# Two groups of products become turns, and four engines get a new order of calls

## The chip, the cores and the metric

The kernel runs on one core of a Trainium2 chip, in one launch. The metric is the device time of that launch in microseconds (us); several runs of the same program are taken, and their median counts. The core has five engines that work side by side, each through its own list of instructions in order: TensorE (PE, which multiplies and transposes into PSUM), VectorE (DVE), ScalarE (ACT), GpSimd (POOL) and SyncE (SP, which here starts transfers). They wait for each other by semaphores.

## The reference

Input x is 16 sequences of 256 tokens of 128 numbers. Two layers follow each other, each on the layer norm of its input, and each added to it:

```
step(params, x):                              # scanned over the 16 sequences
    z, y  = x @ t_k.T, x @ t_v.T
    grads = grad(mean((recon(params, z) - y)**2))     # recon(z) = z + gelu(z @ W1.T + b1) @ W2.T + b2
    params = params - 0.001 * grads
    return params, recon(params, x @ t_q.T)

ffn(x):                                       # each sequence by itself
    x = x + proj(attention(rope(qkv(rmsnorm(x)))))    # 16 heads, 4 of keys, window of 128, a sink
    h2 = rmsnorm(x)
    top 4 of 32 experts per token; x + sum of weight * (silu(h2 @ g) * (h2 @ u)) @ down
```

The parameters go from one sequence to the next, so the steps of the first layer can't run side by side. Everything is in f32.

## The kernel before, in words

After the loads the program has two parts. `layers` runs a loop that is written out over n = -1 to 20; `experts` follows when all engines have left it, and computes the chosen experts over 160 tiles of 128 rows, which GpSimd has sent to DRAM by expert during the loop.

An iteration of the loop works on five sequences at once, each in another stage. Stage F (sequence n) is the step of the first layer: turn the normed rows xn into columns (`x_turn`), `z_products`, `a_products`, then the gradient through `z_rows`, `residual_cols`, `residual_rows`, `hidden_grad` and `gradients`, which DVE's `update` adds to the weights in `fast`, `fast2` and `b1`. Stage O (n - 1) makes the layer's output with the new weights. Stage N (n - 2) makes q, k and v in six chunks (`chunk`, `rope`, `rope_add`, `qk_turn`). Stage A (n - 3) is attention in six units of heads (`scores`, `maxima`, `exps`, `scaled`, `turn_probs`, `take_probs`, `values`, `take_y`); its last units run on into the next iteration. Stage B (n - 4) projects, picks experts and sends rows. All stages are at work from n = 4 to 15, the first ones alone in n = 0 to 2, the last ones alone in n = 16 to 19.

The stages are functions for each engine. What sets the order is `iteration` of each engine: a list of calls, run through from top to bottom. A call waits on semaphores for the calls of other engines that it reads from or whose buffer it takes over, so a call that waits holds up all that stands behind it on its engine. Matrices in the column layout have a token per column (zT, rT, hT2), in the row layout a token per partition (z, r, h). The gradients need z and the residual r in the row layout: `z_rows` (L449) and `residual_rows` (L472) make them in PSUM, and DVE copies them out (`a_rows`, `slope_cdf`). zT is copied out by ACT's `zT_out` (L1176) before `a_products`, rT by `rT_out` (L1196) after `residual_cols`.

`idle` is a product of zeros that PE runs in the first three iterations and the last. `first_stats` makes the statistics of the input on DVE in iteration 0, in passes of four tiles; pass 3 waits for the load of x, pass 4 makes constants. ACT loads a table of functions when it goes from exponentials to Gelu and Tanh and back, twice an iteration.

Of the kernel before, what the change touches and what calls it, by code (L numbers as in the profile page):

```python
# [24 lines left out]
P = 128  # L25
# [201 lines left out]
def layers(m):  # L227
# [12 lines left out]
    with ExitStack() as ctx:  # L240
# [112 lines left out]
        def _(pe):  # L353
# [283 lines left out]
            def iteration(n, par):  # L637
                project(n, par, 1, 0)
                qk_turn(n - 1, 1 - par, 5)
                norm_turn(n - 1, 1 - par)  # L640
                values(n - 1, 1 - par, 4)
                idle(n, par, 0)
                turn_probs(n - 1, 1 - par, 5, 0)
                x_turn(n, par)
                chunk(n, par, 0)
                z_products(n, par)
                idle(n, par, 1)
                idle(n, par, 2)
                scores(n, par, 1)
                turn_probs(n - 1, 1 - par, 5, 1)  # L650
                qk_turn(n, par, 0)
                project(n, par, 1, 1)
                idle(n, par, 3)
                a_products(n, par)
                chunk(n, par, 1)
                values(n - 1, 1 - par, 5)
                turn_probs(n, par, 0, 0)
                scores(n, par, 2)
                turn_probs(n, par, 0, 1)
                z_rows(n, par)  # L660
                qk_turn(n, par, 1)
                project(n, par, 0, 0)
                project(n, par, 0, 1)
                chunk(n, par, 2)
                values(n, par, 0)
                turn_probs(n, par, 1, 0)
                scores(n, par, 3)
                idle(n, par, 4)
                turn_probs(n, par, 1, 1)
                residual_cols(n, par)  # L670
                idle(n, par, 5)
                qk_turn(n, par, 2)
                values(n, par, 1)
                residual_rows(n, par)
                chunk(n, par, 3)
                turn_probs(n, par, 2, 0)
                h2_turn(n, par)
                scores(n, par, 4)
                idle(n, par, 6)
                idle(n, par, 7)  # L680
                turn_probs(n, par, 2, 1)
                hidden_grad(n, par)
                gate(n, par)
                idle(n, par, 8)
                idle(n, par, 9)
                qk_turn(n, par, 3)
                values(n, par, 2)
# [5 lines left out]
                idle(n, par, 10)  # L693
                qk_turn(n, par, 4)
                values(n, par, 3)
                ranks(n, par)
                idle(n, par, 11)
                chunk(n, par, 5)
                turn_probs(n, par, 4, 0)
                scores(n + 1, 1 - par, 0)  # L700
                gradients(n, par)
                turn_probs(n, par, 4, 1)
# [9 lines left out]
        def _(v):  # L712
# [298 lines left out]
            def iteration(n, par):  # L1011
                recips(n - 1, 1 - par, 5)
                scaled(n - 1, 1 - par, 5, 0)
                scaled(n - 1, 1 - par, 5, 1)
                rope(n, par, 0)
# [4 lines left out]
                scaled(n, par, 0, 0)  # L1020
                scaled(n, par, 0, 1)
                sinks(n, par, 1)
                first_stats(n, par, 3)
                rope(n, par, 1)
                first_stats(n, par, 4)
                a_bias(n, par)
                slots(n - 1, 1 - par)
                maxima(n, par, 2)
                shifts(n, par, 2)
                sinks(n, par, 2)  # L1030
                first_stats(n, par, 5)
                sums_out(n, par, 1)
                centred(n, par)
                a_rows(n, par)
                recips(n, par, 1)
                scaled(n, par, 1, 0)
                attended(n, par)
                scaled(n, par, 1, 1)
                rope(n, par, 2)
                sums_out(n, par, 2)  # L1040
                maxima(n, par, 3)
                recips(n, par, 2)
                shifts(n, par, 3)
                sinks(n, par, 3)
                scaled(n, par, 2, 0)
                h2_rows(n, par)
                scaled(n, par, 2, 1)
                first_stats(n, par, 6)
                slope_pdf(n, par)
                slope_cdf(n, par)  # L1050
                rope(n, par, 3)
                sums_out(n, par, 3)
                first_stats(n, par, 7)
                maxima(n, par, 4)
                shifts(n, par, 4)
                first_stats(n, par, 8)
                recips(n, par, 3)
                hidden_grad(n, par)
                pick(n, par)
                sinks(n, par, 4)  # L1060
                first_stats(n, par, 9)
                scaled(n, par, 3, 0)
                scaled(n, par, 3, 1)
                rope(n, par, 4)
                sums_out(n, par, 4)
                maxima(n, par, 5)
                recips(n, par, 4)
                shifts(n, par, 5)
                one_hot(n, par)
                output(n, par)  # L1070
                scaled(n, par, 4, 0)
                scaled(n, par, 4, 1)
                rope(n, par, 5)
                sinks(n, par, 5)
                places(n, par)
                maxima(n + 1, 1 - par, 0)
                first_stats(n, par, 10)
                shifts(n + 1, 1 - par, 0)
                update(n, par)
                normed_rows(n, par)  # L1080
                sinks(n + 1, 1 - par, 0)
                x_norm(n + 1, 1 - par)
# [44 lines left out]
        def _(act):  # L1127
# [122 lines left out]
            def iteration(n, par):  # L1250
                hT_out(n - 1, 1 - par)
                take_y(n - 1, 1 - par, 4)
                sink_terms(n, par, 0)
                xT_out(n, par)
                exps(n, par, 0, 1)
                take_probs(n - 1, 1 - par, 5, 0)
                v_out(n, par, 0)
# [3 lines left out]
                exps(n, par, 1, 0)  # L1261
                sink_terms(n, par, 1)
                v_out(n, par, 1)
                take_y(n - 1, 1 - par, 5)
                exps(n, par, 1, 1)
                take_probs(n, par, 0, 0)
                take_probs(n, par, 0, 1)
                qk_out(n, par, 1)
                exps(n, par, 2, 0)
                exps(n, par, 2, 1)  # L1270
                sink_terms(n, par, 2)
                take_y(n, par, 0)
                gelus(n, par)
                take_probs(n, par, 1, 0)
                take_probs(n, par, 1, 1)
                rT_out(n, par)
                qk_out(n, par, 2)
                sink_terms(n, par, 3)
                exps(n, par, 3, 0)
                exps(n, par, 3, 1)  # L1280
                take_y(n, par, 1)
                take_probs(n, par, 2, 0)
                h2T_out(n, par)
# [4 lines left out]
                weights(n, par)  # L1288
                exps(n, par, 4, 1)
                take_y(n, par, 2)  # L1290
# [4 lines left out]
                take_y(n, par, 3)  # L1295
                exps(n, par, 5, 1)
                take_probs(n, par, 4, 0)
                take_probs(n, par, 4, 1)
                sink_terms(n, par, 5)
                exps(n + 1, 1 - par, 0, 0)  # L1300
                qk_out(n, par, 5)

# [3 lines left out]
        def _(pool):  # L1306
# [81 lines left out]
            def iteration(n, par):  # L1388
                rope_add(n, par, 1)
                send(n, par, 0)  # L1390
                send(n, par, 1)
                rms2(n, par)
                rope_add(n, par, 2)
                rope_add(n, par, 3)
                send(n, par, 2)
# [3 lines left out]
                last_sends(n, par)  # L1399
                send(n, par, 3)  # L1400
                rope_add(n + 1, 1 - par, 0)
                spread(n, par)
# [400 lines left out]
```

## Time and profile before

| | |
|---|---|
| median of three runs | 1043.11 us (1042.41 to 1044.05) |
| the profiled execution's own time | 1046.03 us |
| its span, first to last instruction | 1044.3 us |
| mean granted PE clock | 0.936 |
| PE busy | 888.1 us (85% of the span) |
| DVE, ACT, POOL busy | 684.2, 602.2, 488.0 us |
| loop, to about | 777 us |

The profile is of one execution; "busy" adds up the time in which an engine had an instruction under way. PE works with two sequencer steps that overlap, the load of weights (PEld) and the product (PE). The granted clock is the share of full speed that PE was given: 1.00 is 2.4 GHz, 0.50 is 1.2 GHz. In a list of instructions a row gives start, duration, engine, line, operation, output and inputs, count, and in brackets the idle time ahead of it with what ended it. A row with x4 covers four records.

### The profile page before, as it was taken

Reading aid. Unit: us, or ns where it says so; the run is one execution under the profiler, and the core shown is the slowest. Engines: PE = TensorE matmul, PEld = TensorE weight load, DVE = VectorE, ACT = ScalarE, POOL = GpSimd, SP = SyncE. Lnnn points to the kernel's source line nnn. Section 1 sums busy time; section 2 is a strip of 40 time slices with the busy share of each in tenths; the row PEclk is TensorE's granted clock in tenths of the full one; section 3 lists DMA queues with packets and bytes.
Section 4 is the critical chain, followed back from the end, with each engine's and each line's share of the span. In section 5 each row is a group of like instructions: output and inputs, shape, how many; then the busy total and the mean of one; then the engine's idle time right before and its main releaser. Section 6 shows DMA issues by size and latency. Waiting matters only on the chain. (4 is left out here: it accounts for less than half of the span.)

```text
span 1044.3 us, 21755 instructions
## 1 busy us (share of the span) xinstructions
PE 888.1 (85%) x6865; PEld 674.9 (65%) x6865; DVE 684.2 (66%) x2456; ACT 602.2 (58%) x1987; POOL 488.0 (47%) x643
## 2 busy tenths in 40 slices
PE   3788999999999999999999999999945997777500
PEld 1455777777777777777777777776734886666400
DVE  2645877878788787887877878788742443333208
ACT  1114776767767677676776767877812654444300
POOL 2123313444444443444444444455451777777750
PEclk8788999999999999999999999999966999999855
DMA  6989999999500000000000000000002544432139
GB/s 159 268 273 375 375 374 376 368 370 368 152 13 18 15 10 18 12 18 16 10 17 13 18 15 9 18 18 18 24 33 70 135 133 132 122 105 75 52 110 331
DMA packets 98370, 131.52 MB, mean 126 GB/s; under 512 B 15025, under 2 KB 54866, under 8 KB 98258
## 3 DMA queue, kind: packets, MB, share of 16 engines
q1 hardware_dynamic: 84690, 108.36, 31.5%
q0 software_dynamic: 9216, 19.68, 5.4%
q10 hardware_dynamic: 4352, 2.10, 0.7%
q8 instruction: 57, 0.93, 0.4%
q14 instruction: 55, 0.45, 0.1%
HBM read 30.34 MB, written 99.75 MB: 125 GB/s over the span
## 5 line engine op out<-in xcount | busy, mean ns | idle before, releaser
L1315 POOL TENSOR_TENSOR l_t_cos<-l_t_cos,l_t_sin 128x512 f32<-128x512 f32 (+1 forms) x96 | 104.5, 1088 | 279.3 <-DVE l_t_sin L908 278.6
L1148 ACT ACTIVATE l_prob<-l_score,l_nm 128x128 f32<-128x128 f32 (+1 forms) x512 | 210.3, 432 | 4.1 <-DVE l_nm L767 3.9
L1521 POOL DMA_INDIRECT expert_out<-e_yo,e_dest x160 | 153.7, 960 | 69.4 <-issue 36.9
L756 DVE TENSOR_REDUCE l_mx<-l_score 128x2 f32<-128x512 f32 (+1 forms) x192 | 123.6, 686 | 70.6 <-PE l_score L379 69.0
L94 POOL DMA_INDIRECT expert_rows<-h,slot x128 | 129.6, 1013 | 56.7 <-issue 33.3
L1158 ACT COPY l_probT<-l_turned 128x512 f32<-128x512 f32 x192 | 110.9, 594 | 77.3 <-PE l_turned L393 77.1
L393 PE MATMUL l_turned<-ident_sb,l_prob 128*128 128x128 f32 x768 | 120.8, 283 | 0.4 <-DVE l_prob L741 0.3
L393 PEld LDWEIGHTS l_turned<-ident_sb,l_prob 128*128 128x128 f32 x768 | 83.3, 142 | 48.6 <-issue 43.6
L1148 ACT ACTIVATION_READ_ACCUMULATOR l_prob<-l_score,l_nm 128x1 f32 x512 | 111.3, 217 | 0.0
L379 PE MATMUL l_score<-l_kT,l_qT 64*128 64x128 f32 (+1 forms) x1024 | 110.1, 344 | 0.0
L408 PE MATMUL l_turned<-l_probT,l_vv 128*64 128x128 f32 x1536 | 105.0, 279 | 1.7 <-ACT l_probT L1158 1.5
L408 PEld LDWEIGHTS l_turned<-l_probT,l_vv 128*64 128x64 f32 x1536 | 81.9, 136 | 35.2 <-issue 31.5
L379 PEld LDWEIGHTS l_score<-l_kT,l_qT 64*128 64x128 f32 x1024 | 75.3, 187 | 44.0 <-issue 41.1
L1662 ACT ACTIVATE e_yo<-e_p_y,e_mine 128x128 f32<-128x128 f32 x160 | 45.7, 368 | 88.9 <-DMA expert_out<-e_yo,e_dest 80.1
L555 PE MATMUL l_side_q<-wqkv_sb,l_hT 128*128 128x512 f32 x186 | 96.7, 602 | 0.0
L904 DVE TENSOR_TENSOR l_t_cos<-l_side_q,rope_sb 128x512 f32<-128x512 f32 (+1 forms) x93 | 55.6, 598 | 50.5 <-PE l_side_q L555 50.3
L1603 DVE COPY e_hidT<-e_p_h 128x512 f32<-128x512 f32 x40 | 27.7, 691 | 83.7 <-PE e_p_h L1729 79.1
L1719 PE MATMUL e_p_up<-wup_sb,e_xT 128*128 x320 | 80.1, 396 | 0.0
L741 DVE TENSOR_SCALAR l_prob<-l_prob,l_rec 128x256 f32<-128x256 f32 x256 | 76.0, 354 | 0.6
L1738 PE MATMUL e_p_y<-wdown_sb,e_hidT 128*128 x320 | 45.6, 286 | 31.0 <-ACT e_yo L1662 29.0
L588 PE MATMUL l_side_g<-wproj_sb,l_yT 128*128 128x128 f32 x512 | 66.7, 278 | 0.0
L1719 PEld LDWEIGHTS e_p_up<-wup_sb,e_xT 128*128 128x128 f32 x320 | 60.9, 201 | 7.3
(235 smaller groups left out, 1785.8 us busy)
## 6 DMA issues: line engine op xcount, KB each, us to landing
expert_rows<-zeros SPq DMA_DIRECT2D x32, 2240.0 KB, 22.5
e_xt<-expert_rows SPq DMA_DIRECT2D x160, 70.0 KB
e_rows<-expert_out SPq DMA_DIRECT2D x16, 512.0 KB, 5.9
wup_sb<-in_wup SPq DMA_DIRECT2D x1, 4096.0 KB, 14.5
expert_out<-e_yo,e_dest POOLq DMA_INDIRECT x160
expert_rows<-zeros SPq DMA_DIRECT2D x32, 70.0 KB, 2.2
expert_rows<-zeros SPq DMA_DIRECT2D x4, 560.0 KB, 11.7
expert_rows<-h,slot POOLq DMA_INDIRECT x128, 2.4
```

Of the source, the lines that this page charges most:

```text
L94: m["nc"].gpsimd.indirect_dma_start(m["xs"], bass.IndirectOffsetOnAxis(ap=m["slot"][:, par, c:c + 1], axis=0), m["h2"][:, par, c // TOPK, ...
L379: ins = mm(bank[h][:, i * w:(i + 1) * w], qT[rows, ap, p, tok], kT[rows, ap, g2, 0:w], start=False, stop=(i == len(pairs) - 1))
L393: ins = tr(turned[h][:, k * P:(k + 1) * P], prob[:, u % 2, h, k * P:(k + 1) * P], ident[:])
L408: ins = mm(turned[1][h * DH:(h + 1) * DH, i * P:(i + 1) * P], vv[:, A % 3, k, g * DH:(g + 1) * DH], probT[:, h, blk * P:(blk + 1) * P], st ...
L555: mm(dst[:], hT[:, t * P:(t + 1) * P], m["wqkv"][:, part * 512:(part + 1) * 512], start=False, stop=True).then_inc(s["qkv_ps"], 1)
L741: ins = V.tensor_scalar(prob[:, b, h, j * TOK:(j + 1) * TOK], prob[:, b, h, j * TOK:(j + 1) * TOK], rec[:, b, h, j:j + 1], None, ALU.mult)
L756: V.tensor_reduce(mx[:, b, h, 0:w], score[(2 * u + h) % 3][:].rearrange("p (j k) -> p j k", j=w), AX.X, ALU.max).then_inc(s["mx"], 1)
L1148: ins = A_.activation(prob[:, b, h, cols], score[(2 * u + h) % 3][:, cols], ACT.Exp, bias=nm[:, b, h, j:j + 1], scale=0.125, accum_out=sum ...
L1158: A_.copy(probT[:, h, :], turned[h][:]).then_inc(s["probT"], 1)
L1315: g.tensor_tensor(t_cos[:, c % 2, 0:w], t_cos[:, c % 2, 0:w], t_sin[:, c % 2, 0:w], ALU.add).then_inc(s["added"], 1)
L1521: g_.indirect_dma_start(m["ys"], bass.IndirectOffsetOnAxis(ap=dest[:, g % FOUND, j:j + 1], axis=0), yo[:, g % YO, j, :], None).then_inc(se ...
L1719: ins = mm(p_up[g % 2][:, j, :], xT[:, g % 2, j, :], m["wup"][:, bass.ds(expert(g, j) * (2 * DFF), 2 * DFF)], start=True, stop=True)
```

## The change

`z_rows` and `residual_rows` take the rows from the column layouts that are there already, by turning them (a transpose on PE against the identity), where they were computed a second time by products:

```
@@ z_rows, residual_rows
                 for t in range(TPS):
-                    mm(side_f[:, TOK + t * P:TOK + (t + 1) * P], xnT[:, par, t * P:(t + 1) * P], m["tkT"][:],
-                       start=True, stop=True)
+                    tr(side_f[:, TOK + t * P:TOK + (t + 1) * P], zT[:, 0, t * P:(t + 1) * P], ident[:])
...
                 for t in range(TPS):
-                    dst, tok = side_f[:, TOK + t * P:TOK + (t + 1) * P], slice(t * P, (t + 1) * P)
-                    mm(dst, xnT[:, par, tok], dkvT[:], start=True, stop=False)
-                    mm(dst, hT2[:, 0, tok], fast2[:], start=False, stop=True)
+                    tr(side_f[:, TOK + t * P:TOK + (t + 1) * P], rT[:, t * P:(t + 1) * P], ident[:])
```

The lists of calls of all four engines are in another order. The turn of the iteration is also elsewhere: calls that stood at its head for the sequence before now stand at its end, and the other way round. Of the lists, the rows that the text speaks of:

```
@@ PE, iteration: moved to the end
-                project(n, par, 1, 0)
-                qk_turn(n - 1, 1 - par, 5)
-                norm_turn(n - 1, 1 - par)
-                values(n - 1, 1 - par, 4)
...
                 gradients(n, par)
+                ranks(n, par)
+                values(n, par, 4)
+                qk_turn(n, par, 5)
+                norm_turn(n, par)
+                project(n + 1, 1 - par, 1, 0)
@@ DVE, iteration: x_norm from the end to the head, behind first_stats(n, par, 3)
+                first_stats(n, par, 3)
+                sinks(n, par, 0)
+                x_norm(n, par)
                 recips(n - 1, 1 - par, 5)
...
-                sinks(n + 1, 1 - par, 0)
-                x_norm(n + 1, 1 - par)
@@ POOL, iteration
-                rope_add(n, par, 1)
                 send(n, par, 0)
...
                 rope_add(n + 1, 1 - par, 0)
+                rope_add(n + 1, 1 - par, 1)
```

On PE, in the middle of a full iteration, from the turn of unit 1 to the score of unit 4 (l_turned is a turn of probabilities or, from l_probT, `values`; l_side_q a chunk; l_side_f stage F). Before:

```order
L572 MATMUL l_side_q<-ident_sb,l_t_cos 128x128 x4
L408 MATMUL l_turned1<-l_probT,l_vv 64x128 x8
L479 MATMUL l_side_f<-l_dkvT,l_xnT 128x128
L480 MATMUL l_side_f<-fast2,l_hT2 128x128
L479 MATMUL l_side_f<-l_dkvT,l_xnT 128x128
L480 MATMUL l_side_f<-fast2,l_hT2 128x128
L482 MATMUL l_side_f<-ident_sb,l_hT2 128x128 x2
L357 MATMUL l_side_q<-bias3_bf,ones_bf 128x512
L555 MATMUL l_side_q<-wqkv_sb,l_hT 128x512
L393 MATMUL l_turned0<-ident_sb,l_prob 128x128 x4
L598 MATMUL l_side_g<-ident_sb,h2 128x128 x2
L373 MATMUL l_score2<-mask2,ident_bf 128x512
```

And now, from the turn of unit 1 (its second half) on:

```order
L393 MATMUL l_turned1<-ident_sb,l_prob 128x128 x4
L357 MATMUL l_side_q<-bias3_bf,ones_bf 128x512
L552 MATMUL l_side_q<-wqkv_sb,l_hT 128x512
L393 MATMUL l_turned0<-ident_sb,l_prob 128x128 x4
L408 MATMUL l_turned1<-l_probT,l_vv 64x128 x8
L595 MATMUL l_side_g<-ident_sb,h2 128x128 x2
L477 MATMUL l_side_f<-ident_sb,l_rT 128x128 x2
L479 MATMUL l_side_f<-ident_sb,l_hT2 128x128 x2
L373 MATMUL l_score2<-mask2,ident_bf 128x512
```

The four products of `residual_rows` are two turns of rT, and `h2_turn` (L595) stands between them and `values`.

On ACT, at the head of an iteration, from the copy of xnT to the copies after zT (L1148 and L1145 are `exps`, L1158 and L1155 `take_probs`). Before:

```order
L1174 COPY l_xnT<-l_side_f 128x256 [waits l_xT_ps]
L1148 ACTIVATE l_prob,l_sums<-l_score,l_nm 128x256 [waits l_t_ps,l_nm]
L1148 ACTIVATE l_prob,l_sums<-l_score,l_nm 128x256
L1158 COPY l_probT<-l_turned 128x512 [waits l_y_ps,l_t_ps]
L1218 COPY l_vv<-l_side_q 128x256 [waits l_y_ps,l_sin]
L1182 COPY l_zT<-l_side_f 128x512 [waits l_z_ps]
L1228 COPY l_kT<-l_side_q 128x2x128 [waits l_qk_ps]
L1158 COPY l_probT<-l_turned 128x512 [waits l_y_ps,l_t_ps]
```

And now:

```order
L1171 COPY l_xnT<-l_side_f 128x256 [waits l_xT_ps]
L1164 COPY l_yT<-l_turned 128x2x128 [waits l_y_ps]
L1145 ACTIVATE l_prob,l_sums<-l_score,l_nm 128x256 [waits l_t_ps,l_nm]
L1145 ACTIVATE l_prob,l_sums<-l_score,l_nm 128x256
L1215 COPY l_vv<-l_side_q 128x256 [waits l_y_ps,l_sin]
L1155 COPY l_probT<-l_turned 128x512 [waits l_y_ps,l_t_ps]
L1179 COPY l_zT<-l_side_f 128x512 [waits l_z_ps]
L1225 COPY l_kT<-l_side_q 128x2x128 [waits l_qk_ps]
```

The copy of l_probT for unit 5 has come to stand right ahead of zT; on PE its turn has moved from ahead of `x_turn` to behind `scores(1)`.

On DVE, at the start of iteration 0 (L790 and L787 are `x_norm`, L1088 and L1085 with x_all the statistics). Before:

```order
L790 TENSOR_SCALAR l_xn<-x_all,l_mv,l_rstd 128x128 [waits l_rs0]
L790 TENSOR_SCALAR l_xn<-x_all,l_mv,l_rstd 128x128
L1088 BN_STATS l_stats<-x_all 128x6 [waits x_loaded]
L1088 BN_STATS l_stats<-x_all 128x6 x3
L1091 BN_AGGR l_mv<-l_stats 128x2 [waits l_stat0]
L1091 BN_AGGR l_mv<-l_stats 128x2 x3
```

And now:

```order
L1085 BN_STATS l_stats<-x_all 128x6 [waits x_loaded]
L1085 BN_STATS l_stats<-x_all 128x6 x3
L1088 BN_AGGR l_mv<-l_stats 128x2 [waits l_stat0]
L1088 BN_AGGR l_mv<-l_stats 128x2 x3
L787 TENSOR_SCALAR l_xn<-x_all,l_mv,l_rstd 128x128 [waits l_rs0]
L787 TENSOR_SCALAR l_xn<-x_all,l_mv,l_rstd 128x128
```

`x_norm` of the first sequence stands behind the wait for the whole of x and four tiles of statistics.

## Rows read from the trace of the kernel before

**Rows 1.** Busy time by stretch: iteration 3, iterations 4 to 14, iteration 15.
```profile
core 0: us, PE busy (x) PEld busy (x) DVE busy (x) ACT busy (x) POOL busy (x), PEclk, DMA share, GB/s
91.29:133.10 41.81, 41.34 (x307) 29.30 (x308) 30.25 (x101) 29.14 (x102) 9.35 (x15) 0.93 1.03 375
...
133.10:611.17 478.07, 478.07 (x4018) 361.26 (x4016) 385.54 (x1416) 349.91 (x1200) 213.55 (x308) 1.00 0.34 118
...
611.17:654.63 43.46, 43.46 (x368) 32.83 (x366) 34.70 (x127) 31.81 (x111) 20.23 (x29) 1.00 0.04 14
```

**Rows 2.** Instructions in order of time, PE: `z_rows`, `residual_rows` of iteration 9.
```profile
404.88 0.61 PE L455 MATMUL l_side_f<-tkT_sb,l_xnT 128*128 128x128 f32 x4
405.33 0.38 PE L458 MATMUL l_side_f<-ident_sb,l_aT 128*128 128x128 f32 x2
...
414.85 0.49 PE L479 MATMUL l_side_f<-l_dkvT,l_xnT 128*128 128x128 f32 x2
415.17 0.39 PE L480 MATMUL l_side_f<-fast,l_hT 128*128 128x128 f32 x2
...
415.84 0.38 PE L482 MATMUL l_side_f<-ident_sb,l_hT 128*128 128x128 f32 x2
416.06 0.38 PE L357 MATMUL l_side_q<-bias_bf,ones_bf 128*128 128x512 bf16 x1
```

**Rows 3.** The same view, PE: calls that stand ahead of the two joints.
```profile
397.62 0.65 PE L393 MATMUL l_turned<-ident_sb,l_prob 128*128 128x128 f32 x4
...
398.32 1.06 PE L588 MATMUL l_side_g<-wproj_sb,l_yT 128*128 128x128 f32 x8
399.22 0.60 PE L444 MATMUL l_side_f<-l_zT,fast 128*128 128x256 f32 x2
...
413.82 1.09 PE L408 MATMUL l_turned<-l_probT,l_vv 128*64 128x128 f32 x16
...
417.14 0.60 PE L393 MATMUL l_turned<-ident_sb,l_prob 128*128 128x128 f32 x4
417.57 0.38 PE L598 MATMUL l_side_g<-ident_sb,h 128*128 128x128 f32 x2
417.79 0.59 PE L373 MATMUL l_score<-mask,ident_bf 128*128 128x512 bf16 x2
```

**Rows 4.** The same view, ACT: exponentials, copies and a table load of iteration 9.
```profile
394.56 0.48 ACT L1148 ACTIVATE l_prob<-l_score,l_nm 128x256 f32<-128x256 f32 x1
...
395.47 0.59 ACT L1158 COPY l_probT<-l_turned 128x512 f32<-128x512 f32 x1
...
396.49 0.59 ACT L1182 COPY l_zT<-l_side_f 128x512 f32<-128x512 f32 x1
398.53 0.37 ACT L1228 COPY l_kT<-l_side_q 128x256 f32<-128x256 f32 x1 [1.45 <-PE l_side_q L572]
...
414.54 1.28 ACT L1136 ACT_TABLE_LOAD   x1
415.83 0.21 ACT L1136 ACTIVATE l_es<-l_es 128x4 f32<-128x4 f32 x1
```

**Rows 5.** The same view, iteration 0: DVE, then PE.
```profile
23.76 0.87 DVE L1088 BATCH_NORM_STATS2 l_stats<-x_all 128x6 f32<-128x128 f32 x4 [12.41 <-DMA x_all<-in_x]
24.66 0.38 DVE L1091 BATCH_NORM_AGGREGATE l_mv<-l_stats 128x2 f32<-128x6 f32 x4
...
28.32 0.48 DVE L800 TENSOR_SCALAR l_aT<-l_side_f,b_sb 128x256 f32<-128x256 f32 x1
...
36.89 0.84 DVE L1088 BATCH_NORM_STATS2 l_stats<-x_all 128x6 f32<-128x128 f32 x4
...
38.07 0.19 DVE L851 TENSOR_TENSOR l_da<-l_side_f,l_cdf 128x64 f32<-128x64 f32 x1
...
11.40 0.69 PE L421 MATMUL l_side_f<-ident_sb,l_xn 128*128 128x128 f32 x2 [0.88 <-DVE l_xn L790]
...
14.84 0.82 PE L444 MATMUL l_side_f<-l_zT,fast 128*128 128x256 f32 x2
```

More of the change, by code:

```diff
@@ L646, in iteration @@
                 z_products(n, par)
-                idle(n, par, 1)
-                idle(n, par, 2)
                 scores(n, par, 1)
+                turn_probs(n - 1, 1 - par, 5, 0)
+                idle(n, par, 0)
                 turn_probs(n - 1, 1 - par, 5, 1)
                 qk_turn(n, par, 0)
+                idle(n, par, 1)
                 project(n, par, 1, 1)
-                idle(n, par, 3)
                 a_products(n, par)
                 chunk(n, par, 1)
-                values(n - 1, 1 - par, 5)
                 turn_probs(n, par, 0, 0)
                 scores(n, par, 2)
-                turn_probs(n, par, 0, 1)
-                z_rows(n, par)
+                values(n - 1, 1 - par, 5)
+                idle(n, par, 2)
                 qk_turn(n, par, 1)
                 project(n, par, 0, 0)
+                z_rows(n, par)
+                chunk(n, par, 2)
+                turn_probs(n, par, 0, 1)
                 project(n, par, 0, 1)
-                chunk(n, par, 2)
-                values(n, par, 0)
-                turn_probs(n, par, 1, 0)
+                idle(n, par, 3)
                 scores(n, par, 3)
                 idle(n, par, 4)
+                values(n, par, 0)
+                qk_turn(n, par, 2)
+                turn_probs(n, par, 1, 0)
+                idle(n, par, 5)
+                residual_cols(n, par)
+                idle(n, par, 6)
                 turn_probs(n, par, 1, 1)
-                residual_cols(n, par)
-                idle(n, par, 5)
-                qk_turn(n, par, 2)
+                chunk(n, par, 3)
+                idle(n, par, 7)
+                turn_probs(n, par, 2, 0)
                 values(n, par, 1)
+                h2_turn(n, par)
                 residual_rows(n, par)
-                chunk(n, par, 3)
-                turn_probs(n, par, 2, 0)
-                h2_turn(n, par)
+                idle(n, par, 8)
                 scores(n, par, 4)
-                idle(n, par, 6)
-                idle(n, par, 7)
                 turn_probs(n, par, 2, 1)
+                qk_turn(n, par, 3)
                 hidden_grad(n, par)
                 gate(n, par)
-                idle(n, par, 8)
+                values(n, par, 2)
                 idle(n, par, 9)
-                qk_turn(n, par, 3)
-                values(n, par, 2)
                 chunk(n, par, 4)
@@ L1020, in iteration @@
                 scaled(n, par, 0, 0)
+                first_stats(n, par, 4)
+                sinks(n, par, 1)
                 scaled(n, par, 0, 1)
[L1022 to L1023 removed]
                 rope(n, par, 1)
[L1025 removed]
                 a_bias(n, par)
[L1027 removed]
                 maxima(n, par, 2)
                 shifts(n, par, 2)
+                sums_out(n, par, 1)
                 sinks(n, par, 2)
+                recips(n, par, 1)
+                centred(n, par)
+                scaled(n, par, 1, 0)
+                scaled(n, par, 1, 1)
                 first_stats(n, par, 5)
[L1032 to L1033 removed]
+                rope(n, par, 2)
                 a_rows(n, par)
[L1035 to L1036 removed]
                 attended(n, par)
[L1038 to L1039 removed]
                 sums_out(n, par, 2)
+                recips(n, par, 2)
+                scaled(n, par, 2, 0)
                 maxima(n, par, 3)
[L1042 removed]
                 shifts(n, par, 3)
+                h2_rows(n, par)
+                first_stats(n, par, 6)
                 sinks(n, par, 3)
[L1045 to L1046 removed]
+                slope_pdf(n, par)
+                rope(n, par, 3)
                 scaled(n, par, 2, 1)
[L1048 to L1049 removed]
                 slope_cdf(n, par)
[L1051 removed]
+                maxima(n, par, 4)
+                shifts(n, par, 4)
                 sums_out(n, par, 3)
                 first_stats(n, par, 7)
[L1054 to L1055 removed]
+                hidden_grad(n, par)
                 first_stats(n, par, 8)
+                sinks(n, par, 4)
                 recips(n, par, 3)
[L1058 removed]
                 pick(n, par)
[L1060 to L1061 removed]
                 scaled(n, par, 3, 0)
@@ L1064, in iteration @@
                 rope(n, par, 4)
+                maxima(n, par, 5)
                 sums_out(n, par, 4)
-                maxima(n, par, 5)
+                shifts(n, par, 5)
+                sinks(n, par, 5)
                 recips(n, par, 4)
-                shifts(n, par, 5)
+                scaled(n, par, 4, 0)
+                output(n, par)
+                first_stats(n, par, 9)
+                scaled(n, par, 4, 1)
                 one_hot(n, par)
-                output(n, par)
-                scaled(n, par, 4, 0)
-                scaled(n, par, 4, 1)
                 rope(n, par, 5)
-                sinks(n, par, 5)
-                places(n, par)
                 maxima(n + 1, 1 - par, 0)
-                first_stats(n, par, 10)
                 shifts(n + 1, 1 - par, 0)
                 update(n, par)
+                first_stats(n, par, 10)
                 normed_rows(n, par)
-                sinks(n + 1, 1 - par, 0)
-                x_norm(n + 1, 1 - par)
+                places(n, par)
                 sums_out(n, par, 5)
@@ L1261, in iteration @@
                 exps(n, par, 1, 0)
+                v_out(n, par, 1)
                 sink_terms(n, par, 1)
-                v_out(n, par, 1)
+                exps(n, par, 1, 1)
                 take_y(n - 1, 1 - par, 5)
-                exps(n, par, 1, 1)
+                qk_out(n, par, 1)
                 take_probs(n, par, 0, 0)
+                exps(n, par, 2, 0)
                 take_probs(n, par, 0, 1)
-                qk_out(n, par, 1)
-                exps(n, par, 2, 0)
+                sink_terms(n, par, 2)
                 exps(n, par, 2, 1)
-                sink_terms(n, par, 2)
+                gelus(n, par)
                 take_y(n, par, 0)
-                gelus(n, par)
+                qk_out(n, par, 2)
                 take_probs(n, par, 1, 0)
+                rT_out(n, par)
                 take_probs(n, par, 1, 1)
-                rT_out(n, par)
-                qk_out(n, par, 2)
+                exps(n, par, 3, 0)
+                take_probs(n, par, 2, 0)
+                take_y(n, par, 1)
+                h2T_out(n, par)
                 sink_terms(n, par, 3)
-                exps(n, par, 3, 0)
                 exps(n, par, 3, 1)
-                take_y(n, par, 1)
-                take_probs(n, par, 2, 0)
-                h2T_out(n, par)
                 take_probs(n, par, 2, 1)
@@ L1287, in iteration @@
                 sink_terms(n, par, 4)
-                weights(n, par)
+                take_y(n, par, 2)
                 exps(n, par, 4, 1)
-                take_y(n, par, 2)
                 take_probs(n, par, 3, 0)
@@ L1295, in iteration @@
                 take_y(n, par, 3)
+                weights(n, par)
+                take_probs(n, par, 4, 0)
+                sink_terms(n, par, 5)
+                take_probs(n, par, 4, 1)
                 exps(n, par, 5, 1)
-                take_probs(n, par, 4, 0)
-                take_probs(n, par, 4, 1)
-                sink_terms(n, par, 5)
                 exps(n + 1, 1 - par, 0, 0)
                 qk_out(n, par, 5)
+                hT_out(n, par)
             run(iteration, 1, 1)
@@ L1388, in iteration @@
             def iteration(n, par):
[L1389 removed]
                 send(n, par, 0)
                 send(n, par, 1)
+                rope_add(n, par, 2)
                 rms2(n, par)
[L1393 removed]
+                send(n, par, 2)
+                last_sends(n, par)
                 rope_add(n, par, 3)
[L1395 removed]
                 rope_add(n, par, 4)
```

20 lines of the change are left out of this document (8 added, 12 removed).

## The prediction

> **What bounds the kernel now.** I read three views in this order: busy time per stretch, then the list of instructions in order of time on PE, then the same list on ACT and DVE. In the first [rows 1] the reader is to compare the length of a stretch with the busy time of PE in it. From 133.10 to 611.17 us, which is eleven iterations of 43.46 us, PE is busy for 478.07 of 478.07 us at a granted clock of 1.00 (2.4 GHz). DVE is busy for 385.54 of them and ACT for 349.91. The iteration n = 15 that follows is the same (43.46 of 43.46), and n = 3 before it has PE busy for 41.34 of 41.81 us at a mean clock of 0.93. So in thirteen iterations (n = 3 to 15) nothing ends later than PE, and its time is the number of its instructions times their spacing. A microsecond of PE work that goes there is a microsecond of the whole, until another engine is late. In the second view [rows 2] the spacing is to be read as the difference of two start times; the durations overlap, since matmuls are pipelined. Iterations 0 to 2 wait on chains of engines, and after about 757 us the kernel is the last sequence's chain and the expert stage, which the change doesn't touch.
>
> **The products that become turns.** An f32 product shows as two PE records, a turn as one. In `z_rows` the two products (4 records) take 404.88 to 405.33 = 0.45 us; in `residual_rows` the four products (8 records) take 414.85 to 415.84 = 0.99. Two turns take 415.84 to 416.06 = 0.22 [rows 2]. The change puts two turns in place of each group: 0.45 - 0.22 = 0.23 and 0.99 - 0.22 = 0.77, together 1.00. Of that about 0.10 doesn't go: the first pair of `residual_rows` takes 415.17 - 414.85 = 0.32 against 0.22 for a usual pair, because `values` stands ahead of it, and now `h2_turn` stands behind that `values` and will pay it. So 0.90 an iteration, times 13 = 11.7 us; bounds 0.80 (10.4) and 1.00 (13.0). The waits that the two calls have are older than what they replace: `z_rows` now reads zT, which ACT wrote before `a_products`, and `residual_rows` reads rT, for which it waited before.
>
> **The new order in the thirteen iterations.** It costs nothing as long as each PE wait is met. I laid PE's new calls one after another with their spacings and asked of each wait whether its producer, at the durations of the rows, is done. Most have a microsecond or more. Two joints on ACT are tight, and they are what I price.
>
> Joint 1, at the head: ACT's `zT_out` now stands behind `take_probs(5, 0)`, which waits for the turn of unit 5. After that turn PE has another turn, `qk_turn` and `project` before `a_products` wants zT; the same three take 397.62 to 399.22 now, 1.60 us [rows 3]. ACT needs about 0.2 to start (`qk_turn` gives way to `project` at 398.32, and ACT's copy of its result starts at 398.53), 0.59 for the copy and 0.59 for zT, 1.38 in all [rows 3, 4]. 0.2 remains. Behind `zT_out` on ACT are `qk_out(0)` and the next `take_probs`, so a late one there delays `chunk(1)` as well.
>
> Joint 2, in the middle: `scores(4)` wants `exps(3, 0)`, ahead of which ACT now has `take_probs(1, 1)` and the table load that stood at `sink_terms(3)`. Between the turn and `scores(4)` PE has `chunk` (416.06 to 417.14, 1.08), a turn (417.14 to 417.57, 0.43), `values` (413.82 to 414.85, 1.03), `h2_turn` (0.22) and four turns (0.44): 3.20 us [rows 2, 3]. ACT needs 0.2 + 0.59 + 1.28 for the load + 0.91 for the two exponentials (394.56 to 395.47) = 2.98 [rows 4]. Again 0.2 remains.
>
> The Trainium skill's page "ScalarE: Activation LUTs", section "What ACT_TABLE_LOAD costs", speaks against this joint: it gives the load as 1.28 us and a drain of 1.38 beside it, 2.66 together. By that, an estimate from the page, ACT would need 4.36 us and PE would wait 1.16 in each iteration. The trace agrees with the load (1.28) and shows no drain behind it: load at 414.54, next ACTIVATE at 415.83 [rows 4].
>
> A few more joints (hn to `norm_turn`, hT to `x_turn` at the turn of the iteration, `take_y(3)` to the turn of unit 4) look alike, so some will miss by a tenth. I take 0.1 us an iteration, +1.3; bounds 0 and 0.5 (+6.5), the latter if several miss by what they seem to have. `rope_add(1)` now stands ahead of four sends on POOL's queue; POOL is busy for 20.23 of 43.46 [rows 1] and the sends have an iteration to land, so nothing. DVE's calls are the same in number; with some 8 us free in an iteration it has cover. No call on SP's queue moves.
>
> **The first iterations.** In iteration 0, `x_norm` used to run before DVE's wait for x, which ends at 23.76 us; now the wait, and four tiles' statistics, stand ahead of it. The chain from the turn of xn to the end of `a_products` (11.40 to 14.84 + 0.82, so 4.3 us) lay under that wait and now comes after it [rows 5]. xn would be ready at about 24.66 + 0.4 + 0.5 = 25.6, `a_products` at about 29.7 with one filler product fewer ahead of it, against `a_bias` at 28.32 now: 1.3 us late. On the other side a pass of 1.2 us of statistics (36.89 to 38.07) moves from ahead of the product that makes `da` to behind it, and with a shorter pass moved behind `update` it gives 1.2 or more back. I take 0, bounds -1.5 and +1.5. In iterations 1 and 2 the two calls stand on the chain that PE waits for: 0.9 each, -1.8; bounds 0 and -3.6 (at the lower clock level, 1.2 GHz, the records take twice as long). The last iterations (16 to 19) have neither call; the other order there I take as 0, 1.0 either way.
>
> **Sum**, against the profiled execution of 1046.03 us (span 1044.3 and 1.7 around it): -11.7 + 1.3 + 0 - 1.8 + 0 = -12.2, so 1033.8. The median of the runs is 2.92 below the profiled time, so 1043.1 - 12.2 = 1030.9; I say 1031.
>
> **The rivals.** (a) The tight joints miss by half a microsecond together in each iteration: +6.5 in place of +1.3, 1036. For it: two joints with 0.2 us each; against it: a late producer shifts the whole ring of engines once, and the gaps are kept afterwards.
> (b) A stretch at the lower clock level more. Iteration 3 has a mean clock of 0.93 over 41.81 us [rows 1], so some 2.9 us lost; another such stretch in the first iterations, where the fillers stand elsewhere, gives 1034. Against it: eleven iterations run at 1.00 although most of their records are short.
> (c) Slower: joint 1 fails as a whole. `turn_probs(5, 0)` waits for DVE's `scaled(5, 0)`, which now stands behind `sinks`, `x_norm` and `recips` of the new iteration; if that is late, the turn, ACT's copy, zT, `a_products` and the chain of the fast weights are late one behind the other, and again in the next iteration. It decides from 0.94 us per iteration (12.2 / 13); at 1.5 us it gives 1031 - 1.3 + 19.5 = 1049. Against it: DVE has those 8 us free, and PE has four other calls ahead of the turn in the new iteration.
> (d) The table load with a wait behind it, as joint 2 would have it with a load of twice the length: about 1.2 us per iteration, 1031 - 1.3 + 15 = 1045, a little slower. Against it: the row above.
> (e) PE's records are fewer, but the loop takes as long because a chain over DVE and ACT (maxima, exponentials, turns, values) sets it: 1043. Against it: PE waits nowhere in those iterations, while DVE and ACT do.
>
> **How the numbers follow.** Forecast (1025 to 1034) 0.66; (a) 0.12; (b) 0.08; (c) 0.06; (d) 0.03; (e) 0.05. Two per mille, 2.1 us, is about what a measurement of this kernel can tell from no change. Faster: forecast, (a), (b) and a little of (e): 0.87; the same: 0.04; slower: (c) and (d): 0.09. The best ends of all terms give -13.0 - 1.5 - 3.6 - 1.0 = -19, 1024; the worst end -10.4 + 6.5 + 1.5 + 1.0 = -1.4, 1041.7. I cut both ends and go from 1025 to 1037, which leaves out (c), (d), (e) and the worst of (a).
>
> **What would show it.** In the changed kernel the middle iterations take about 42.6 us, from one turn of xn to the next, with PE busy for nearly all of it; both groups show 32 records of turns where 64 and 128 of products stood. Waits of PE before `a_products`, `scores(4)`, `norm_turn` or the turn of xn show (a), (c) or (d), and name which. In iteration 0 the turn of xn is at about 25.6 us. The forecast is wrong if the middle iterations keep 43.4 us, or if PE waits there by more than half a microsecond an iteration.

## The result, and the profile after

The changed kernel takes 1020.91 us in the median (1020.22 to 1022.59), against 1043.11; the ratio is 0.9783 [0.9770, 0.9796]. That is 22.2 us less, where 12.1 were foretold: the direction was right, the size was not, and the time lies below the range. The profiled executions differ by 25.1 us in their span (1044.3 and 1019.2).

Busy time by stretch of the changed kernel (iteration 2, iteration 3, iterations 4 to 14, iteration 15; a stretch goes from one turn of xn to the next), to be held against [rows 1]:

```profile
core 0: us, PE busy (x) PEld busy (x) DVE busy (x) ACT busy (x) POOL busy (x), PEclk, DMA share, GB/s
60.77:86.18 25.41, 22.88 (x112) 14.21 (x113) 15.92 (x49) 8.48 (x20) 9.10 (x15) 0.94 0.96 340
86.18:124.12 37.94, 37.13 (x295) 26.68 (x295) 31.20 (x100) 28.79 (x101) 9.62 (x15) 1.00 1.03 375
124.12:588.41 464.29, 463.94 (x3929) 355.86 (x3928) 409.32 (x1415) 346.96 (x1200) 227.28 (x311) 1.00 0.37 129
588.41:630.65 42.24, 42.21 (x358) 32.54 (x359) 36.93 (x128) 31.66 (x111) 21.18 (x28) 1.00 0.05 15
```

PE is still busy for the whole of the middle, and eleven iterations take 464.29 / 11 = 42.21 us each instead of 43.46: 1.25 less, where the prediction had 0.8. Iteration 3 lost 3.9 us, and the granted clock there is 1.00 instead of 0.93.

The two groups of turns in the changed kernel, PE in order of time (start, duration, line), against [rows 2]:

```profile
389.38 0.38 PE L455 MATMUL l_side_f<-ident_sb,l_zT 128*128 128x128 f32 x2
389.60 0.38 PE L457 MATMUL l_side_f<-ident_sb,l_aT 128*128 128x128 f32 x2
389.82 0.38 PE L357 MATMUL l_side_q<-bias_bf,ones_bf 128*128 128x512 bf16 x1
...
398.67 1.09 PE L408 MATMUL l_turned<-l_probT,l_vv 128*64 128x128 f32 x16
399.69 0.44 PE L595 MATMUL l_side_g<-ident_sb,h 128*128 128x128 f32 x2
399.97 0.38 PE L477 MATMUL l_side_f<-ident_sb,l_rT 128*128 128x128 f32 x2
400.19 0.38 PE L479 MATMUL l_side_f<-ident_sb,l_hT 128*128 128x128 f32 x2
```

Two turns take 0.22 us in both places, as foretold, and `h2_turn` behind `values` takes 399.97 - 399.69 = 0.28 instead of 0.22. So what was worked out of the products holds, but for one price: `h2_turn` pays 0.06 for standing behind `values`, where 0.10 was foretold. What was not in the sum is seen at `values` and `scores`. Before, they stood like this:

```profile
400.08 0.38 PE L357 MATMUL l_side_q<-bias_bf,ones_bf 128*128 128x512 bf16 x1
400.30 1.02 PE L555 MATMUL l_side_q<-wqkv_sb,l_hT 128*128 128x512 f32 x2
401.25 1.09 PE L408 MATMUL l_turned<-l_probT,l_vv 128*64 128x128 f32 x16
402.28 0.66 PE L393 MATMUL l_turned<-ident_sb,l_prob 128*128 128x128 f32 x4
402.77 0.38 PE L373 MATMUL l_score<-mask,ident_bf 128*128 128x512 bf16 x1
...
403.29 1.16 PE L379 MATMUL l_score<-l_kT,l_qT 64*128 64x128 f32 x16
404.39 0.66 PE L393 MATMUL l_turned<-ident_sb,l_prob 128*128 128x128 f32 x4
```

And in the changed kernel, the first of two places where `values` now stands right behind `scores`:

```profile
385.46 0.59 PE L373 MATMUL l_score<-mask,ident_bf 128*128 128x512 bf16 x2
385.99 1.16 PE L379 MATMUL l_score<-l_kT,l_qT 64*128 64x128 f32 x16
387.08 1.09 PE L408 MATMUL l_turned<-l_probT,l_vv 128*64 128x128 f32 x16
388.10 0.44 PE L569 MATMUL l_side_q<-ident_sb,l_t_cos 128*128 128x128 f32 x2
388.38 0.22 PE L357 MATMUL l_side_g<-bias_bf,ones_bf 128*128 128x128 bf16 x1
```

The differences of the starts are to be read. The call ahead of `values` pays: `chunk` takes 400.08 to 401.25 = 1.17 us here, and 416.06 to 417.14 = 1.08 ahead of a turn [rows 2, 3], 0.09 less. The call behind pays too: four turns take 0.49 behind `values` (402.28 to 402.77), and 0.43 elsewhere (417.14 to 417.57, [rows 3]). The trace gives the operand of `scores` as 64*128 and that of `values` as 128*64, that of the others as 128*128; by these rows a step between the two kinds costs 0.09 on the way into `values` and about 0.06 on the way out. `scores` is no different: the two mask products ahead of it take 385.46 to 385.99 = 0.53 where one product of that width takes 0.22 (400.08 to 400.30), and four turns behind it take 0.49 (404.39 to 404.88, [rows 2]). But where `values` follows `scores` directly, `scores` takes no longer for it (385.99 to 387.08 = 1.09, and 403.29 to 404.39 = 1.10 ahead of turns in the trace of before), and nothing is left behind `scores` to pay its way out. The old order has six paid steps into `values` in an iteration, the new one four, and two paid steps out of `scores` fewer: 2 x 0.09 + 2 x 0.06 = 0.3 us. This is an account from spacings; the experiments ask whether it is right.

The Trainium skill's page "TensorEngine Tiling (Array Packing)", section "Tiling Modes", under "Key Properties", says that changing the tiling mode drains TensorE. It gives no price; the rows above agree with it at 0.09 and 0.06 us. From 64*128 to 128*64 the mode changes too, and no price is seen there.

### The profile page after: what moved, and what is told of

The parts are those of the page before. It is cut to its first block and busy times, and to the rows that moved or that the text cites. A ratio compares the mean times of both kernels' runs of the same rounds, so it can differ in the third digit from the quotient of the medians.

```text
span 1019.2 us, 21500 instructions
## 1 busy us (share of the span) xinstructions
PE 867.9 (85%) x6737; PEld 668.7 (66%) x6737; DVE 711.4 (70%) x2456; ACT 597.6 (59%) x1987; POOL 505.0 (50%) x643
## 5 line engine op out<-in xcount | busy, mean ns | idle before, releaser
L1312 POOL TENSOR_TENSOR l_t_cos<-l_t_cos,l_t_sin 128x512 f32<-128x512 f32 (+1 forms) x96 | 115.0, 1198 | 249.6 <-DVE l_t_sin L905 249.5
L1145 ACT ACTIVATE l_prob<-l_score,l_nm 128x128 f32<-128x128 f32 (+1 forms) x512 | 211.8, 435 | 19.2 <-DVE l_nm L764 18.9
L1155 ACT COPY l_probT<-l_turned 128x512 f32<-128x512 f32 x192 | 111.4, 593 | 67.4 <-PE l_turned L393 65.0
L393 PEld LDWEIGHTS l_turned<-ident_sb,l_prob 128*128 128x128 f32 x768 | 88.0, 141 | 47.9 <-issue 41.8
L1145 ACT ACTIVATION_READ_ACCUMULATOR l_prob<-l_score,l_nm 128x1 f32 x512 | 112.7, 220 | 0.0
L393 PE MATMUL l_turned<-ident_sb,l_prob 128*128 128x128 f32 x768 | 110.3, 276 | 1.3 <-DVE l_prob L738 0.6
L1716 PE MATMUL e_p_up<-wup_sb,e_xT 128*128 x320 | 83.2, 407 | 0.0
L585 PE MATMUL l_side_g<-wproj_sb,l_yT 128*128 128x128 f32 x512 | 69.2, 278 | 0.0
L1716 PEld LDWEIGHTS e_p_up<-wup_sb,e_xT 128*128 128x128 f32 x320 | 63.3, 209 | 8.1
```

The lines of the kernel that those rows point to most:

```text
L393: ins = tr(turned[h][:, k * P:(k + 1) * P], prob[:, u % 2, h, k * P:(k + 1) * P], ident[:])
L1145: ins = A_.activation(prob[:, b, h, cols], score[(2 * u + h) % 3][:, cols], ACT.Exp, bias=nm[:, b, h, j:j + 1], scale=0.125, accum_out=sum ...
L1155: A_.copy(probT[:, h, :], turned[h][:]).then_inc(s["probT"], 1)
L1312: g.tensor_tensor(t_cos[:, c % 2, 0:w], t_cos[:, c % 2, 0:w], t_sin[:, c % 2, 0:w], ALU.add).then_inc(s["added"], 1)
L1716: ins = mm(p_up[g % 2][:, j, :], xT[:, g % 2, j, :], m["wup"][:, bass.ds(expert(g, j) * (2 * DFF), 2 * DFF)], start=True, stop=True)
```

## Experiments

Two theories were set against each other first. S: the turns save what the spacing says in any order, and the new order saves about 0.3 us an iteration by itself, through its neighbours of `values`. R: the turns make the whole gain, by more than their spacing.

**The turns alone, in the old order.**

```
 z_rows:         - mm(side_f[..], xnT[:, par, ..], m["tkT"][:], start=True, stop=True)
                 + tr(side_f[..], zT[:, 0, ..], ident[:])
 residual_rows:  - mm(dst, xnT[:, par, tok], dkvT[:], ..); mm(dst, hT2[:, 0, tok], fast2[:], ..)
                 + tr(side_f[..], rT[:, ..], ident[:])
 (the order of every engine as before)
```

Expected: 

> Order of before, with the two groups of turns alone. Theory S (spacing): the turns save what their records' spacing says, 0.94 us an iteration (0.23 in z_rows, 0.71 to 0.77 in residual_rows), whatever the order, and the new order saves about 0.3 more by itself. Then the middle iterations take 42.5 us and the whole is 13 x 0.95 + 1.8 = 14 us shorter than before, about 1029; the stretch at the lower clock level that before shows at 90 to 97 us stays. Rival R: the turns make the whole gain, and the order none: middle iterations 42.2, 1021. Rival I (the turns need the new order, since rT or zT would come late in the old one): PE waits before residual_rows, iterations near 43, 1036.

Measured: 1028.31 us, ratio 0.9838 [0.9784, 0.9892]. Iteration 3, then iterations 4 to 14:

```profile
84.92:125.74 40.82, 39.70 (x295) 28.16 (x300) 30.09 (x101) 28.93 (x102) 9.33 (x15) 0.93 1.03 375
125.74:593.83 468.09, 465.08 (x3875) 351.48 (x3929) 385.83 (x1416) 349.53 (x1201) 213.48 (x308) 1.00 0.36 126
```

468.09 / 11 = 42.55, so 0.91 an iteration, next to the 0.90 of the prediction. R and I fall. The lower clock in iteration 3 stays (0.93).

**The order alone, with the products.**

```
 (the four lists of calls as after; z_rows and residual_rows as before)
```

Expected: 

> Order of after, with the six products in place of the four turns. Theory S: PE waits nowhere, and two calls of values stand right behind scores, so PE changes two times less an iteration into the half-array products of values (0.094 us each by the spacing of the record ahead) and two times less out of scores and values (0.056 each): 0.3 us an iteration, middle iterations 43.2, 15 x 0.3 = 4.5 us, and 3 to 5 more if the stretch at the lower clock level at 90 to 97 us is gone by the order: 1034 to 1039. Rival R (the turns make it all): 1043, middle iterations 43.46. Rival P (what the prediction said, the order costs 0.1 an iteration): 1044.

Measured: 1035.26 us, ratio 0.9907 [0.9874, 0.9941]:

```profile
87.86:126.23 38.37, 37.47 (x300) 27.72 (x304) 30.77 (x100) 28.83 (x101) 9.62 (x15) 1.00 1.03 375
126.23:600.70 474.47, 468.73 (x3962) 365.80 (x4016) 410.28 (x1415) 347.35 (x1200) 226.97 (x311) 1.00 0.36 125
```

474.47 / 11 = 43.13, so 0.33 less than before by the order alone, and 0.91 + 0.33 = 1.24 of the 1.25. Theory S has the size, and what the prediction said of the order (P) falls. Iteration 3 is 38.4 us at a clock of 1.00.

**The kernel before, profiled again.** Expected: 

> The kernel before, profiled a second time. Theory O (the lower clock level at 90 to 97 us belongs to the order of before): it is there again, and iteration 3 takes 41.7 us again. Rival Z (it is a chance of one execution; the profiled time was 2.9 us above the median): it is gone, iteration 3 takes about 38.8, and the time is near 1043.

Measured: 1044.4 us, span 1042.6. Iterations 2 and 3:

```profile
62.18:91.70 29.52, 24.29 (x118) 16.05 (x120) 15.81 (x49) 8.47 (x20) 9.10 (x15) 0.90 1.01 364
91.70:132.21 40.51, 39.39 (x303) 28.79 (x308) 30.27 (x101) 29.04 (x102) 9.34 (x15) 0.96 1.03 375
```

Neither expectation was met in full: the fall of the clock in iteration 3 is there again, but shorter (0.96 in place of 0.93), and so is the iteration, by 1.3 us.

**The two places undone.**

```
 PE:  scores(n, par, 2)                       scores(n, par, 3)
    - values(n - 1, 1 - par, 5)             - values(n, par, 0)
      qk_turn(n, par, 1)                      qk_turn(n, par, 2)
    + values(n - 1, 1 - par, 5)             + values(n, par, 0)
 (the rest as after)
```

Expected: 

> After, with qk_turn moved in between scores and values at both places (unit 5 of the iteration ahead, and unit 0). Theory S: the first costs 0.094 + 0.056 - 0.045 = 0.10 and the second 0.094 + 0.056 = 0.15 us an iteration, 0.25 together, middle iterations 42.48, 14 x 0.25 = 3.5 us: 1024.5. Rival N (the step between the calls costs nothing, and the new order gains by something else): 1021, iterations 42.23. Rival Q: qk_turn, now 1 us earlier, waits for POOL's rotations (rope_add): over 0.3 us an iteration more, with the wait shown before qk_turn.

Measured: 1025.39 us (1024.36 to 1027.07, above all runs of after), ratio 0.9811 [0.9765, 0.9857]. Iterations 4 to 14, and the first place:

```profile
122.79:590.53 467.74, 462.02 (x3874) 355.06 (x3927) 410.77 (x1415) 349.47 (x1200) 226.90 (x311) 1.00 0.37 129
```
```profile
386.58 1.16 PE L379 MATMUL l_score<-l_kT,l_qT 64*128 64x128 f32 x16
387.68 0.44 PE L569 MATMUL l_side_q<-ident_sb,l_t_cos 128*128 128x128 f32 x2
388.05 1.09 PE L408 MATMUL l_turned<-l_probT,l_vv 128*64 128x128 f32 x16
389.07 0.23 PE L357 MATMUL l_side_g<-bias_bf,ones_bf 128*128 128x128 bf16 x1
```

The two turns at 387.68 now take 0.37 us, between `scores` and `values`, against 0.28 at 388.10 in the changed kernel: the 0.09 of the step. 467.74 / 11 = 42.52, 0.31 more than after (0.25 expected; of the rest some 0.04 is a small wait of `qk_turn` at the second place, where `scores` ahead of it takes 393.45 to 394.55 = 1.10 instead of 1.06; rival Q had it in kind). So exchanging neighbours at two places, with the same instructions on every engine, costs nearly as much as the whole order had gained in a middle iteration. That it is the step between array halves, and not another property of these neighbours, is argued from the rows; that it is the neighbours is shown.

**More of the same: units 2 and 3, then all units behind `scores`.**

```
 two more:  gate, idle(9), chunk(4), scores(5), values(2), turn_probs(3, 0), output, turn_probs(3, 1),
            qk_turn(4), chunk(5), turn_probs(4, 0), scores(n + 1, 0), values(3), gradients,
            turn_probs(4, 1), qk_turn(5), norm_turn, ranks, values(4)
 all six:   the same, and scores(4), values(1) and scores(n, 1), values(n - 1, 4)
 (ACT: take_y, take_probs and exps moved to suit)
```

Expected of two more: 

> After, with two more calls of values put right behind scores (unit 2 behind scores(5), unit 3 behind scores(0) of the next iteration), and on ACT take_y(2) and take_y(3) moved behind the exponentials that scores waits for. Theory S (what a call of values costs beyond its products is set by the call ahead of it): 0.094 less at each entry and 0.01 less at each exit, 0.21 an iteration, middle iterations 42.02, 14 x 0.21 = 3 us: 1018 against after's 1021. Rival N (adjacency is worth nothing here): 42.23, 1021. Rival W (values now later than the turns that wait for its result): PE waits before turn_probs(3, 1) or turn_probs(4, 1), shown in the trace; 0.3 an iteration or more, 1022 or above.

Expected of all six: 

> After, with all six calls of values right behind a call of scores, and ACT's calls moved to suit. Theory S: unit 1 saves 0.15, units 2 and 3 0.10 each, unit 4 0.13: 0.48 an iteration, middle iterations 41.75, 14 x 0.48 = 6.7 us: 1014. Rival N: 42.23, 1021. Rival W: the turn of the second half of a unit's probabilities waits for ACT's take_y of the unit ahead, now late; it decides if these waits are over 0.48 an iteration together, then 1021 or above, with PE's waits before turn_probs named in the trace.

Measured: 1043.4 us, ratio 0.9992 [0.9983, 1.0001], and 1082.32 us, ratio 1.0359 [1.0345, 1.0373]; iterations of 43.45 and 46.01 us. The waits of PE in iterations 4 to 14 of the first and of the second (in total, times, longest):

```profile
PE l_side_q L357 <- ACT l_qT L1228: 8.0, 11, 0.7
PE l_side_f L534 <- DVE l_hn L870: 3.8, 11, 0.4
```
```profile
PE l_side_q L357 <- ACT l_qT L1228: 20.8, 22, 1.2
PE l_score L373 <- ACT l_prob L1145: 9.3, 11, 0.9
PE l_side_g L357 <- DVE l_place L979: 3.5, 11, 0.3
PE l_side_f L534 <- DVE l_hn L870: 3.0, 12, 0.3
```

Rival W is right that waits eat the gain, but not where it put them: not the turns behind `take_y` wait, but `chunk` for ACT's copy of q and k (`qk_out`) and `norm_turn` for hn, which both orders also put ahead of `values(4)`, nearer to `gradients`. PE was the bound by a small margin only.

**One more: unit 3.**

```
 PE:  qk_turn(4), turn_probs(4, 0), scores(n + 1, 0), values(3), chunk(5), gradients, turn_probs(4, 1),
      ranks, norm_turn, values(4), qk_turn(5), project(n + 1, 1, 0)
 ACT: exps(5, 0) ahead of qk_out(4), exps(5, 1) ahead of take_y(3)
```

Expected: 

> After, with one call of values more right behind scores: unit 3 behind scores(0) of the next iteration, chunk(5) behind that, and exps(5, 0) ahead of qk_out(4) on ACT. Theory S: 0.094 less at the entry and 0.056 less at the exit of scores, middle iterations 42.08, 14 x 0.15 = 2 us: 1019 against after's 1021, if no wait comes. Rival W: scores(0) now stands 2 us earlier and waits for ACT's exps(5, 0), or chunk(5) for qk_out(4); more than 0.15 an iteration and it is no gain: 1021 to 1025, with that wait in the trace.

Measured: 1065.16 us, ratio 1.0197 [1.0179, 1.0215]. Iterations 4, 5 and 6, and what PE waited for from iteration 4 to 14:

```profile
128.78:175.34 46.56, 44.75 (x360) 34.29 (x359) 36.41 (x126) 31.64 (x109) 13.34 (x21) 0.94 1.03 375
175.34:221.94 46.60, 44.73 (x359) 33.98 (x358) 36.74 (x129) 31.60 (x109) 22.07 (x29) 0.95 1.03 370
221.94:266.41 44.47, 42.60 (x357) 32.34 (x357) 36.87 (x129) 31.63 (x110) 21.70 (x29) 1.00 1.03 365
```
```profile
PE l_side_f L534 <- DVE l_hn L870: 17.0, 11, 1.5
PE l_turned L393 <- DVE l_prob L738: 3.1, 11, 0.4
```

The wait is another one again: `norm_turn`, which this order puts ahead of `values(4)` and so 1.1 us nearer to `gradients`, waits 1.5 us for hn in every iteration. That is more than the 0.15 to be gained, and more than I allowed. No version beyond the changed kernel came out of these.

**The changed kernel again.** Expected: 

> The kernel after, profiled and timed a second time beside the others. By theory O (no stretch at the lower clock level between the first 64 us and the last sequence in this order): again none there, iteration 3 about 38 us, middle iterations 42.23, 1021. If the clock there was chance: a stretch at 80 to 100 us, and iteration 3 at 39 to 41 us.

Measured: 1021.05 us, ratio 0.9769 [0.9754, 0.9785], span 1019.7. Iterations 2 and 3:

```profile
59.79:86.80 27.01, 24.47 (x112) 15.00 (x112) 15.94 (x49) 8.47 (x20) 9.11 (x15) 0.89 0.93 328
86.80:124.76 37.96, 37.12 (x295) 26.67 (x296) 31.20 (x100) 28.83 (x101) 9.62 (x15) 1.00 1.03 375
```

Iteration 3 is at 1.00 again, as in the order alone and in the kernel with the two places undone; the three profiles of the old order (two of before, one with the turns) show 0.93, 0.96 and 0.93. That part belongs to the order.

## Why the prediction was wrong, by its own steps

The two second profiles (spans 1042.6 and 1019.7) stand 22.9 us apart, like the medians, so the sum is told by them (us from the span's start):

| Stretch | before | after | measured | foretold |
|---|---|---|---|---|
| start to the turn of xn of iteration 1 | 42.2 | 41.1 | -1.1 | 0 |
| iterations 1 and 2 | 49.5 | 45.7 | -3.8 | -1.8 |
| iteration 3 | 40.5 | 38.0 | -2.5 | -0.8 |
| iterations 4 to 14 | 478.1 | 464.3 | -13.8 | -8.8 |
| iteration 15 to the end | 432.3 | 430.6 | -1.7 | -0.8 |
| sum | 1042.6 | 1019.7 | -22.9 | -12.2 |

- **What bounds the kernel**: right in the main: PE's records set the middle in both kernels. "PE waits nowhere" was not quite so. Records overlap, so a wait of a tenth shows neither in the busy time nor as idle time, only in the spacing. In before the chunk ahead of the turn of unit 4 takes 428.56 to 429.73 = 1.17 with no `values` behind it, where 1.08 is its usual time, and the turn 0.46 instead of 0.43:

```profile
428.56 0.38 PE L357 MATMUL l_side_q<-bias_bf,ones_bf 128*128 128x512 bf16 x1
429.73 0.63 PE L393 MATMUL l_turned<-ident_sb,l_prob 128*128 128x128 f32 x4
430.19 0.59 PE L373 MATMUL l_score<-mask,ident_bf 128*128 128x512 bf16 x2
```

  With two other calls such small waits come to about 0.2 us an iteration in the old order; they are gone in the new one. What this turn waits for the trace doesn't name.
- **The products**: right, 0.90 foretold and 0.91 measured by the turns alone. That it fits to a hundredth is luck: with 0.06 in place of 0.10 behind `values` the spacing gives 0.95, and 0.04 of it went into the small waits of the old order, which grew.
- **The new order in the thirteen iterations**: this step failed. It said that the order "costs nothing as long as each PE wait is met", took +0.1 an iteration and let the range go from 0 to +0.5. Measured is -0.33 (the order alone), thus 0.43 an iteration, some 5 us of the missing 10.7. I laid PE's new calls one after another with the spacing that each had in the old order, as if it belonged to the call; it belongs to a call and its neighbour. The row that says so was in hand: the first pair of `residual_rows` behind `values` takes 0.32 against 0.22 [rows 2]. I carried it over to `h2_turn` and didn't ask how many such steps the new order has. The waits, which the 0.1 stood for, were of the right kind: the one at the turn of xn (below) costs 0.2 an iteration, and about as much is won by the small waits that are gone. So the gain of the order is that of the steps. And a bound of 0 on the side of a gain had no reason behind it.
- **The joints**: right as far as they go. Neither joint 1 nor joint 2 shows a wait in the middle iterations. On ACT the table load of joint 2 is followed at once by the exponentials, as [rows 4] had it and against the drain of the Trainium skill's page "ScalarE: Activation LUTs" ("What ACT_TABLE_LOAD costs"), so (d) fell:

```profile
397.87 1.28 ACT L1145 ACT_TABLE_LOAD   x1
399.17 0.47 ACT L1145 ACTIVATE l_prob<-l_score,l_nm 128x256 f32<-128x256 f32 x1
```

  The only wait left there is where hT meets the turn of xn; `project` ahead of it takes 1.15 us (376.12 to 377.27) in place of 0.95:

```profile
376.12 1.11 PE L585 MATMUL l_side_g<-wproj_sb,l_yT 128*128 128x128 f32 x8
377.27 0.41 PE L421 MATMUL l_side_f<-ident_sb,l_xn 128*128 128x128 f32 x2
```

- **The clock in iteration 3** (rival b): looked at from one side only. I asked what one stretch more at 1.2 GHz would cost, not what one less would give. In before PE waited 1.35 us for POOL's rotation ahead of a `qk_turn`, and the granted clock fell at 90.4 us, just as the next wait, 0.83 for hT, began:

```profile
89.58 0.66 PE L572 MATMUL l_score<-ident_sb,l_t_cos 128*128 128x128 f32 x4 [1.35 <-POOL l_t_cos L1315]
90.08 0.38 PE L537 MATMUL l_side_f<-ident_sb,l_hn 128*128 128x128 f32 x2
91.29 0.69 PE L421 MATMUL l_side_f<-ident_sb,l_xn 128*128 128x128 f32 x2 [0.83 <-ACT l_hT L1210]
```

  A mean of 0.93 over 41.8 us is 5.8 us at half the speed, 2.9 lost; 0.96 over 40.5 is 1.6 lost. Both give 38.9 without the fall, and 38.0 of after is 0.9 below that. The longest wait for the rotation in iteration 2 is 1.3 to 1.4 us in the three profiles of the old order and 0.5 to 0.8 in the seven of the new order and its variants. But unit 3's kernel waits 1.2 us for hn at the end of iteration 2, and its clock stays at 1.00 up to 125 us, so the length of one wait alone doesn't decide. That such waits made the clock fall is read from their place in time, not tried.
- **The first iterations**: too small, by 3.1 us with the head. I left the products of iteration 0 out of the sum, and took 0.9 for iterations 1 and 2 although my own bound had twice that. The turns alone shorten the head by 2.0 us, iterations 1 and 2 by 2.2 and 2.1; the order alone shortens the head by 0.9 and iteration 2 by 3.2, and makes iteration 1 0.7 longer. These don't add up to the 4.9 of both, the clock there differs from run to run, and how they share it stays open. The turn of xn of iteration 0, foretold for 25.6, is at 25.2 and 25.7.
- **The last iterations**: -0.5 beside iteration 15, within the bound of 1.
- The other rivals, (a), (c), (d) and (e), didn't come. (The 1.2 us of (d) was also mis-summed: a load of twice the length gives 2.98 + 1.28 - 3.20 = 1.06.) The mechanism of the largest part was none of them: an order that changes the price of its records by their neighbours.

## What to carry to other kernels

Where PE is the bound and hardly waits, an order still has a price: count the steps between kinds of matmul (half-array and full-array here), and take a record's cost from rows with the same neighbours. Small waits are to be read there too, since busy time hides them. Bound a reordering on both sides, and the same for the clock: a stretch that the old order spends at the lower level can go as well as come. And once such steps are gone from the places where data is ready, the next exchange buys a wait: 0.15 to 0.5 us of spacing was paid with waits of 0.3 to 1.5 us on ACT and DVE in each of the three attempts here.

## What the runs showed of the hardware

A call of f32 matmuls with a half-array operand makes the full-array call ahead of it 0.09 us longer and turns behind it 0.06, at a granted clock of 1.00 (a pair of f32 products behind it 0.10, [rows 2]); between two half-array calls that follow each other, `scores` and then `values`, both prices are gone. What in the engine takes this time isn't shown by these runs.

The clock can fall in the middle iterations too: in unit 3's kernel, where PE waits 1.5 us for hn in each iteration, the mean granted clock of iterations 4 and 5 is 0.94 and 0.95 and they take 46.6 us, and iteration 6, with the same wait, runs at 1.00 (2.4 GHz) and takes 44.5. What tells them apart isn't shown.
